# One bank of the maxima's ring becomes a third bank of scores in every chunk; the rows of ones and the masks are issued elsewhere

## The reference, cut to what matters

```python
qh = (q @ Wq.T + bq).reshape(B, L, H, E)        # 16 heads of 16, q = layernorm(x)
kh = (k @ Wk.T + bk).reshape(B, S, H, E)        # k = v = ctx, S = 1601
vh = (v @ Wv.T + bv).reshape(B, S, H, E)
scores = jnp.einsum('blhe,bshe->bhls', qh, kh)
scores = scores * tau[:, None, None, :] + delta[:, None, None, :]
a = jax.nn.softmax(scale * scores, axis=-1)
out = jnp.einsum('bhls,bshd->blhd', a, vh).reshape(B, L, D)
return out @ Wo.T + bo
```

## Time and profile before

| | before |
|---|---|
| median of 3 runs | 1050.87 us (1049.43 to 1054.49) |
| the profiled execution | 1050.86 us, its span 1048.8 us |
| TensorE busy | 968.5 us, 92% of the span |
| TensorE's weight loads busy | 386.0 us, 37% |
| VectorE busy | 745.7 us, 71% |
| ScalarE busy | 571.2 us, 54% |
| GpSimd busy | 67.8 us, 6% |
| start, projections and first maxima | 0 to 94 us |
| chunk 0 | 94 to 255 us |
| chunks 1, 2, 3 | 255 to 481, 481 to 709, 709 to 927 us |
| layers behind the last chunk, output | 927 to 1048.8 us |

### The profile page before, as it was taken

The page is one execution under the profiler, slowest core; times in us unless marked ns, Lnnn a source line. Parts: engine busy times, 40 slices in busy tenths (PEclk is TensorE's granted clock), DMA queues, the critical chain, the costliest instruction groups (busy, mean ns, idle before and its releaser), DMA issues.

```text
span 1048.8 us, 13626 instructions
## 1 busy us (share of the span) xinstructions
PE 968.5 (92%) x4794; PEld 386.0 (37%) x4794; DVE 745.7 (71%) x1704; ACT 571.2 (54%) x1063; POOL 67.8 (6%) x98
## 2 busy tenths in 40 slices
PE   6789999999999989999999999999999989789986
PEld 3454232232333333433333334323333334234633
DVE  4779888888778877776788877866788673226634
ACT  2355676666655456576545456666554466730330
POOL 4252000000000000000000000001000000100000
PEclk8899999999999999999999999999999899999999
DMA  7834700001000000001000000001000000040032
GB/s 190 192 80 100 141 17 16 1 17 36 1 17 0 16 1 1 17 1 56 1 16 1 16 1 16 1 23 34 3 13 1 1 1 21 21 130 1 1 100 81
DMA packets 34444, 36.19 MB, mean 35 GB/s; under 512 B 7021, under 2 KB 31386, under 8 KB 34116
## 3 DMA queue, kind: packets, MB, share of 16 engines
q1 hardware_dynamic: 32810, 34.05, 12.6%
q0 software_dynamic: 512, 0.77, 0.3%
q10 hardware_dynamic: 1054, 0.51, 0.3%
HBM read 21.55 MB, written 7.35 MB: 28 GB/s over the span
## 4 chain that ended last, share of the span: by engine, by line
issue 59%; PE 26%; DVE 5%; ACT 3%; POOL 3%; DMA 2%; SPq 1%; POOLq 1%; DVEq 0%; ACTq 0%
PE ps_m L1109 6%; PE ps_o L1193 6%; PE ps_e L1395 4%; PE ps_e L1066 2%; DVE mx L1696 2%; PE ps_m L1395 1%; DMA xres<-in_x 1%; SPq L578 1%; PE ps_m L1213 1%; POOL rstd L714 1%; ACT probs L892 1%; POOL xres L777 1%; DMA x<-xres 1%; PE ps_e L1207 1%; PE ps_o L1144 0%
## 5 line engine op out<-in xcount | busy, mean ns | idle before, releaser
L1696 DVE TENSOR_REDUCE mx<-ps_m 128x1 f32<-128x401 f32 x1024 | 533.5, 568 | 151.0 <-PE ps_m L1109 143.9
L892 ACT ACTIVATE probs<-ps_e 128x512 f32<-128x512 f32 (+1 forms) x763 | 437.2, 598 | 302.0 <-PE ps_e L1395 299.7
L1109 PE MATMUL ps_m<-k_stack,q_stack 99*128 99x401 bf16 x1024 | 307.6, 340 | 15.2 <-DVE mx L1696 12.7
L1395 PE MATMUL ps_e<-q_stack,k_stack 101*128 101x512 bf16 (+1 forms) x763 | 295.8, 389 | 23.2 <-ACT probs L892 20.9
L1193 PE MATMUL ps_o<-probs,v_heads 128*32 128x512 f32 (+1 forms) x1664 | 224.1, 611 | 0.0
L1395 PEld LDWEIGHTS ps_e<-q_stack,k_stack 101*128 101x128 bf16 (+1 forms) x763 | 75.3, 99 | 280.2 <-ACT probs L892 200.6
L1109 PEld LDWEIGHTS ps_m<-k_stack,q_stack 99*128 99x128 bf16 x1024 | 101.5, 99 | 158.5 <-DVE mx L1696 104.5
L1297 PE MATMUL ps_m<-expert_w,xnT 128*128 128x512 f32 x192 | 98.5, 593 | 0.6 <-DVE xb L1834 0.4
L1193 PEld LDWEIGHTS ps_o<-probs,v_heads 128*32 128x32 f32 (+1 forms) x1664 | 33.1, 108 | 59.5 <-issue 48.4
L892 ACT ACTIVATE probs<-ps_m 128x512 f32<-128x512 f32 (+1 forms) x69 | 41.5, 601 | 16.0 <-PE ps_m L1395 14.8
L1834 DVE SCALAR_TENSOR_TENSOR xb<-ps_m,hot,xb 128x256 f32<-128x256 f32 x84 | 40.6, 483 | 8.3 <-issue 0.5
(11 more groups left out here) (337 smaller groups left out, 731.1 us busy)
## 6 DMA issues: line engine op xcount, KB each, us to landing
q_stack<-q_parts SPq DMA_DIRECT2D x78, 64.0 KB, 2.6
expert_w<-in_expert_wT SPq DMA_DIRECT2D x2, 1024.0 KB, 12.8
xres<-in_x SPq DMA_DIRECT2D x4, 512.0 KB, 3.8
x<-xres SPq DMA_DIRECT2D x4, 512.0 KB, 3.0
probs<-x SPq DMA_DIRECT2D x1, 2048.0 KB, 8.5
k_stack<-alphaT SPq DMA_DIRECT2D x10, 200.1 KB, 7.7
probs<-in_ctxT SPq DMA_DIRECT2D x3, 512.0 KB, 9.5
q_parts<-probs SPq DMA_DIRECT2D x4, 384.0 KB, 2.5
```

The lines of the kernel that those rows point to most:

```text
L892: act.activation(probs[0:n, k % 2, h, :], score_bank(c, k, h)[0:n, :], ACT.Exp).then_inc(s["exp_done"], 1)
L1109: pe.matmul(ring_bank((n1, u))[:, 0:SPLIT], qst[0:MAX_ROW, g, h, P * t:P * t + P], kst[0:MAX_ROW, HG * g + h, QUARTER_START[q]:QUARTER_STA ...
L1395: pe.matmul(score_bank(c, k, h)[0:n, :], kst[0:ROWS, HG * g + h, P * st:P * st + n], qst[0:ROWS, g, h, :], start=True, stop=True).then_inc ...
L1696: dve.tensor_reduce(mx[:, q, col:col + 1], ring_bank((n1, u))[:, 0:SPLIT], AX.X, ALU.max)\
```

## The change

RING becomes 2. Bank 2 of `ps_m` goes to the scores, in all four chunks, and every QK waits for the exponentials of the one three before it. `FIRST_JOB` = 3 keeps the other layers' banks where they were. The DMA of the rows of ones moves from GpSimd's queue to ScalarE's, behind the four loads there. `masks()` is cut in three steps, at units 4, 10 and 16. Fifteen numbers of `BY_LOAD` change by one to three.

```diff
-RING = 3
+RING = 2
+FIRST_JOB = 3
...
-BESIDE = [(8, ("U",))]
+BESIDE = [(6 * i + 4, ("U", i)) for i in range(3)]
...
-BY_LOAD = [4, 5, 3, 7, 5, 2, 2, 7, 7, 3, 6, 4, 7,
+BY_LOAD = [5, 5, 3, 7, 5, 2, 2, 7, 7, 3, 4, 6, 6,
...
-        ps_m = ps("ps_m", [P, RING + 2, CT])
+        ps_m = ps("ps_m", [P, FIRST_JOB + 2, CT])
+        ps_s = (*ps_e, ps_m[:, RING, :])
...
-            return ps_e[h % 2] if c else (*ps_e, ps_x)[(HG * k + h + 1) % 3]
+            return ps_s[(HG * (SLOTS * c + k) + h) % 3]
...
-            pool.wait_ge(s["consts_set"], 1)
-            pool.dma_start(qst[DELTA_ROW:DELTA_ROW + 3, :, :, :].rearrange("p g h t -> p g (h t)"),
-                           ones_sb[0:3, :].unsqueeze(1).broadcast_to((3, NG, HG * CT))).then_inc(s["ld_ones"], 16)
...
+            act.wait_ge(s["consts_set"], 1)
+            act.dma_start(qst[DELTA_ROW:DELTA_ROW + 3, :, :, :].rearrange("p g h t -> p g (h t)"),
+                          ones_sb[0:3, :].unsqueeze(1).broadcast_to((3, NG, HG * CT))).then_inc(s["ld_ones"], 16)
...
-                        need(pe, s["exp_done"], HG * SLOTS * c + HG * k + h - (1 if c else 2))
+                        need(pe, s["exp_done"], HG * SLOTS * c + HG * k + h - 2)
```

More of the change, by code:

```diff
@@ L220 @@
 HALF_JOB = {name: divmod(i, 2)[::-1] for i, name in enumerate(HALF_JOBS)}
-HALF_BANKS = ((RING, 0), (RING + 1, 1))
+HALF_BANKS = ((FIRST_JOB, 0), (FIRST_JOB + 1, 1))
 HT = TT // 2
@@ L228, in out_bank @@
 def out_bank(c, i):
-    return (0, RING)[(c + (c == NC - 1 and i)) % 2]
+    return (0, FIRST_JOB)[(c + (c == NC - 1 and i)) % 2]
 def rows_of(st):
@@ L386, in build @@
         ps_e = [ps(f"ps_e{i}", [P, CT]) for i in range(2)]
-        ps_m = ps("ps_m", [P, RING + 2, CT])
+        ps_m = ps("ps_m", [P, FIRST_JOB + 2, CT])
         ps_o = ps("ps_o", [P, CT])
-        ps_x = ps_m[:, RING + 1, :]
+        ps_x = ps_m[:, FIRST_JOB + 1, :]
+        ps_s = (*ps_e, ps_m[:, RING, :])
         names = """ld_const ld_masks ld_early ld_cond ld_encwin ld_expert ld_delta delta_stored ld_delta_k ld_ones ld_fill ld_k ld_slot
@@ L419, in bank @@
         def bank(job, c):
-            return ps_m[:, RING + JOB[job, c][0], :]
+            return ps_m[:, FIRST_JOB + JOB[job, c][0], :]
         def bank_free(eng, job, c):
@@ L534, in v_psum @@
         def v_psum(i):
-            return ps_m[0:rows_of(i), i % RING, 0:D] if i < V_EARLY else ps_o[0:rows_of(i), 0:D]
+            return ps_m[0:rows_of(i), i % FIRST_JOB, 0:D] if i < V_EARLY else ps_o[0:rows_of(i), 0:D]
         def block_cols(b):
@@ L874, in step @@
                     act.wait_ge(s["xnT_psum"], args[0] + 1)
-                    act.copy(xnT[:], ps_m[:, RING:RING + 2, :]).then_inc(s["xnT_ready"], 1)
+                    act.copy(xnT[:], ps_m[:, FIRST_JOB:FIRST_JOB + 2, :]).then_inc(s["xnT_ready"], 1)
                 if kind == "M":
@@ L1134, in step @@
                         for t in range(TT):
-                            mm = pe.transpose(ps_m[:, RING + k, P * t:P * t + P], xn[:, t, P * k:P * k + P], ident[:])
+                            mm = pe.transpose(ps_m[:, FIRST_JOB + k, P * t:P * t + P], xn[:, t, P * k:P * k + P], ident[:])
                     mm.then_inc(s["xnT_psum"], 1)
@@ L1657, in condition, with masks @@
                 dve.drain()
[L1659 to L1674, removed]
+            def masks(i):
+                if i == 0:
+                    dve.wait_ge(s["ld_masks"], 32)
+                    dve.tensor_scalar(iota_w[:], iota_w[:], win_f[:, 7:8], None, ALU.add)
+                    dve.tensor_reduce(slot_mean[:], slotT[:], AX.X, ALU.add)
+                    dve.tensor_copy(bv_rows, bv_cols.unsqueeze(2).broadcast_to((P, KT, P)))
+                    dve.drain()
+                    dve.tensor_scalar(slot_mean[:], slot_mean[:], 1.0 / NS, None, ALU.mult).then_inc(s["mean_ready"], 1)
+                if i == 1:
+                    dve.tensor_scalar(keep[:], iota_w[:], win_f[:, 5:6], None, ALU.is_ge)
+                    dve.tensor_scalar(gauss[:], iota_w[:], win_f[:, 6:7], None, ALU.is_le)
+                    dve.drain()
+                    dve.tensor_scalar(iota_w[:], iota_w[:], cond_pt, None, ALU.subtract)
+                if i == 2:
+                    dve.drain()
+                    dve.tensor_tensor(keep[:], keep[:], gauss[:], ALU.mult)
+                    dve.drain()
+                    dve.tensor_scalar(neg_mask[:], keep[:], -1.0, BIG, ALU.add, ALU.mult)
+                    dve.tensor_tensor(iota_w[:], iota_w[:], iota_w[:], ALU.mult).then_inc(s["masks_ready"], 1)
             def stats(src):
@@ L1729, in step @@
                 if kind == "U":
-                    masks()
+                    masks(args[0])
                 if kind == "u":
```

## The result

The changed kernel takes 1114.78 us (median of 4 runs, 1113.80 to 1117.58) against 1050.34 us for the kernel before on the same chip: a ratio of 1.062 (1.060 to 1.064). That is 64 us slower. The forecast was 40 us slower, 1091 us, with a range up to 1110 us: the sign was right, the size was not. The profiled execution has a span of 1113.7 us against 1048.8 us, so 64.9 us have to be found in it.

The account below looks back on a forecast made before the run. The prediction took TensorE's order, with its short waits, to set the end. Its terms, 24 + 36 - 20 + 0 = +40 us on 1050.86 us, gave 1091 us, with an 8 in 10 range of 1064 to 1110 us.

Parts of the forecast that it names:

- Ring of two in chunk 0: Chunk 0: units wait for reductions with two banks, slots grow from 2.99 to 3.50 us; +24 us, between 20 and 28.
- Ring in chunks 1 to 3: Chunks 1 to 3: units wait for banks beside expert products and in slots with a pair; +36 us, from +17 to +48.
- 0.56 us of an expert slot: Slots beside an expert product: two unit waits, +0.42 and +0.14 us, in 30 slots; 16.8 us.
- of such slots with a pair, in other mixes, there are 55: Chunks 1 to 3: 55 other slots with paired units, each losing 0.35 us as in one seven-unit slot; 19.3 us.
- one bank less in reserve at three steps of VectorE: Before chunk 0: costs 0.5 us at each of three VectorE steps, part of a +3.5 us loss.
- Third bank of scores: Chunks 1 to 3: the third QK no longer waits for the first exponential; -20 us, at the lower end -10.
- 42 gains of 0.48 us: Chunks 1 to 3: 42 slots with two QKs side by side, each 0.48 us shorter, 2.46 instead of 2.94 us.
- Ahead of chunk 0: The start: +3.5 us from the smaller ring, -3.5 us from masks in three steps; net 0, between -5 and +4.
- `BY_LOAD` and the ones: The load table only shifts units between neighbouring slots; the rows of ones are issued in ScalarE's idle time, costing nothing.
- Rival 3: Chunk 0: short waits make the granted clock fall five times, 2.8 us each, giving 1105 us; chance 0.06.
- Rival 2: Chunks 1 to 3: scores' bank returns half, both pairs of a slot pay; +62 us, 1113 us; chance 0.10.

## Why the forecast was right in sign and short in size

- **Ring of two in chunk 0, +24:** +25.7 us in the changed kernel, +25.8 with the ring alone. Slots of 3.52 us where 3.50 were forecast, and the seven slots with transposes were not cheaper, as had been assumed, but paid 0.53 to 0.68 us. (Five reductions in 2.50 us start 0.48 us apart, not 0.50, as the last record is 0.57 us long; it changes little.)
- **Ring in chunks 1 to 3, +36:** mis-sized, +50.8 us alone. The 0.56 us of an expert slot held (0.58). The step that failed is "of such slots with a pair, in other mixes, there are 55": one number, 0.35 us, was put on all of them, read from a slot beside which VectorE had nothing else to do. The prediction priced "one bank less in reserve at three steps of VectorE" ahead of chunk 0, and left the same steps out behind it. There are seven slots a chunk at or behind which VectorE makes means or normalises (1.38 us, plus up to 1.5 us of waiting for GpSimd), and the 21 cost 15.0 us. Eleven of them hold a pair and stood in the sum at 3.9 us, the other ten at nothing. The 43 other slots with a pair cost 18.1 us instead of 15.1. And the clock, which the sum had at nothing, was 17.1 us longer at half in these chunks, some 5 to 7 us of the 50.8 by the price below (an estimate); by the same price the 21.2 us more in the 21 slots are 6 to 9 of their 15.0.
- **Third bank of scores, -20:** -10 us. The short slots are 2.46 us long as forecast, and outside the 21 slots the bank gives 16 us; inside, it gives 3 us in the short ones and takes 9 us back in those behind them. The failed step is that 42 gains of 0.48 us were added up as if TensorE's stream alone set the end. Where VectorE's step ends at a time of its own, arriving sooner only lengthens the wait.
- **Ahead of chunk 0, 0:** -1.4 us, which is less than this stage varies from profile to profile (90.7 to 94.0 us in the seven kernels with this start and the ring of two). That it came out near 0 is luck: both halves were too small and cancel. The new start gives 7.7 us with three banks, and the ring of two takes 6.3 us of them.
- **`BY_LOAD` and the ones, nothing:** shown for the table. The ones were not tried alone; their issue takes 0.92 us of ScalarE's queue, and its first copy of keys starts at 11.19 instead of 10.89 us.
- **The clock.** Rival 3 was given 0.06, and it is part of what happened. Two slots of the same kind within one profile (the changed kernel with four banks in chunk 0), the first without, the second with a fall of the clock:

```profile
512.40:518.63 6.23, 4.58 (x31) 1.89 (x28) 5.53 (x12) 2.87 (x6) 0.14 (x1) 1.00 0.00 0
...
757.71:765.37 7.66, 6.01 (x32) 2.67 (x28) 5.57 (x12) 2.96 (x6) 0.20 (x1) 0.78 0.00 0
```

They differ by 1.43 us, for 3.4 us at the lower level; 0.42 us for each us there. Another pair, the 28th slots of chunks 1 and 2 of the kernel before, gives 0.3 (3.42 and 4.46 us). By that the 20.5 us more at half clock in chunks 1 to 3 are some 6 to 9 us of the 41.3 (an estimate). Of the 37.5 us of the changed kernel 35.1 lie in the 21 slots named above, and 13.0 of the 17.0 before. In chunk 0, where TensorE waits 0.7 us a slot more than its stream needs, but in short pieces, the clock keeps 1.00. That a clock falls in a kernel that cycles through banks is what the Trainium skill tells (TensorE: Matmul & The Clock Gate, "A second HAM failure mode: psum-queue depth-cycling"). It speaks of short idle times between groups; in this trace those of chunk 0 went with a clock of 1.00. What exactly makes the clock fall stays open. Many falls came behind the long waits at `normal`, but others came without one (411.95 above), a wait of 1.44 us in the kernel before went without a fall (385.98), and in the kernel with `normal` two places later the long wait was gone from these slots (0.88 us was left), and it fell all the same, one slot further on. Of the gain of 16.7 us without the wait for `rstd`, 23.9 us less at the lower level make some 7 to 10, and the wait itself the rest, 7 to 10 us; this rests on the same price and was not measured apart. It is near the 6.1 us that the same wait has in the slots of the kernel before.

Rival 2's sum was 62 us, 2 us from the time that came out. Its halves were near too: the score bank returned half, and the ring cost 51 us against its 48. But that is luck: its reason was ScalarE late with copies, and where the gain was lost TensorE waits for the maxima of L1702. It had been given 0.10.

## What to carry to other kernels

A buffer of a ring is worth the wait that it ends in the regular slots, and also the reserve that it is where the consumer does something else; count every step of the consumer that is longer than the ring is deep, with what that step itself waits for. A gain ahead of a point where another engine sets the time is no gain: follow the first place where two engines meet behind it, and see which of them came last. Look at the clock before you read a time: an edit can end a wait and show no gain, because the clock was lower in that run of slots. And look for a resource that is idle in one phase only: banks without a user in chunk 0 gave more than moving one between two users in all chunks.

## What the runs showed of the hardware

A bank is back 1.00 us after its unit has started, if VectorE stands ready, before and after the change: 0.37 us to the reduction, 0.57 us of it, 0.06 us to the next unit. GpSimd's step of four numbers to a power takes 1.02 us on 128 x 4 elements, and from the end of the means to VectorE's first use of `rstd` it is some 1.5 us (304.81 to 306.29), longer than any reduction. A wait of TensorE of 1.54 us was followed by 3.4 us at half clock, starting 1.4 us after TensorE had gone on (308.21, 309.60), in the same slot; with `normal` two places later the fall stood in the slot behind (310.00 to 317.13 at 0.79). A us at half clock cost 0.3 to 0.42 us of time. In the kernel before, an edit that took 6.1 us off eight slots came with 17 us more at half clock and the same time.
